# Gated cross-attention: the attention sums turned by VectorE in 32x32 blocks instead of by TensorE

## The reference

```python
Q = query @ Wq.T + bq; K = key @ Wk.T + bk; V = value @ Wv.T + bv      # 16 heads of 16
dot = einsum('bhsd,bhtd->bhst', Q, K) / sqrt(16)
out = einsum('bhst,bhtd->bhsd', softmax(dot), V)
out = out.reshape(B, T_src, D_MODEL)        # [head, token, 16] is read as [token, 256] as it lies
return out @ Wh.T + bh
x = x + tanh(g_xattn[0]) * attention(layernorm(x), ctx)
x = x + tanh(g_ffn[0]) * ffn(layernorm(x))  # w1, w3, silu, w2 plus two experts of rank 16 per token
```

## Time and profile before

| | us |
|---|---|
| median of 3 runs | 506.98 (505.81 to 508.72) |
| the profiled execution | 509.6 |
| its span in the trace | 507.7 |
| PE busy | 487.7 (96%) |
| DVE busy | 357.9 (70%) |
| ACT busy | 266.6 (53%) |
| POOL busy | 282.4 (56%) |

### The profile page before, as it was taken

One profiled execution on the slowest core, in us unless ns is written; L12 is line 12 of the kernel. 1 busy time (PEld: TensorE's weight loads), 2 busy tenths in 40 slices (PEclk: granted clock), 3 DMA queues, 4 the chain that ended last, 5 costly groups with the idle time before them and its releaser, 6 DMA issues.

```text
span 507.7 us, 11754 instructions
## 1 busy us (share of the span) xinstructions
PE 487.7 (96%) x4350; PEld 456.2 (90%) x4350; DVE 357.9 (70%) x768; ACT 266.6 (53%) x584; POOL 282.4 (56%) x339
## 2 busy tenths in 40 slices
PE   7888999999999999999899999999999999999996
PEld 6657999999999999997789999899999999999994
DVE  6866777877878877888577869856486456854444
ACT  4456766666676777667666533443335333233331
POOL 5645666666666666561676536644386444854440
PEclk9989999999999999999989999999999999999999
DMA  7793786677777777553601000010000100001001
GB/s 199 180 289 93 216 214 153 157 182 190 189 179 180 180 176 169 120 111 57 204 10 17 1 0 1 1 34 0 1 0 2 34 1 1 0 2 34 0 1 32
DMA packets 51144, 45.83 MB, mean 90 GB/s; under 512 B 33935, under 2 KB 40115, under 8 KB 51088
## 3 DMA queue, kind: packets, MB, share of 16 engines
q1 hardware_dynamic: 41310, 23.18, 19.6%
q0 software_dynamic: 7504, 18.69, 14.1%
q10 hardware_dynamic: 2274, 3.21, 2.0%
HBM read 20.59 MB, written 6.66 MB: 54 GB/s over the span
## 4 chain that ended last, share of the span: by engine, by line
PE 84%; DVE 6%; DMA 5%; issue 2%; ACT 2%; POOL 1%; ACTq 0%; DVEq 0%
PE bank L1368 14%; PE bank L1223 7%; PE bank L1246 7%; PE bank L1372 7%; PE bank L1385 6%; PE bank L1420 6%; PE bank L1205 6%; PE bank L1259 6%; PE bank L1193 5%; PE bank L1400 4%; DMA QS<-crow 3%; PE bank L1292 3%; PE bank L1403 2%; PE bank L1180 2%; PE bank L1335 2%
## 5 line engine op out<-in xcount | busy, mean ns | idle before, releaser
L970 DVE TENSOR_REDUCE nmax<-bank 100x1 f32<-100x361 f32 x256 | 130.0, 529 | 38.4 <-PE bank L1223 33.4
L419 POOL TENSOR_TENSOR awl<-hb,awh 128x400 fp32r<-128x400 f32 x63 | 70.2, 1114 | 109.4 <-ACT awh L627 109.4
L529 ACT ACTIVATE pt<-bank 120x400 f32<-120x400 f32 (+1 forms) x192 | 90.3, 503 | 25.8 <-PE bank L1246 12.2
L627 ACT ACTIVATE awh<-hb 128x400 fp32r<-128x400 f32 x64 | 34.5, 539 | 119.0 <-DVE hb L906 118.7
L1223 PE MATMUL bank<-KS,QS 96*100 96x362 f32 x256 | 86.9, 358 | 5.2 <-DVE nmax L970 4.8
L899 DVE TENSOR_TENSOR hb<-sil,bank 128x400 f32<-128x400 f32 x64 | 36.5, 570 | 73.7 <-PE bank L1385 37.9
L1246 PE MATMUL bank<-QS,KS 97*120 97x200 f32 (+1 forms) x384 | 66.4, 271 | 1.6 <-ACT pt L529 1.0
L1246 PEld LDWEIGHTS bank<-QS,KS 97*120 97x120 f32 (+1 forms) x384 | 60.2, 184 | 2.8 <-DMA QS<-crow 1.7
L328 POOL TENSOR_TENSOR cth<-craw,cth 128x724 fp32r<-128x724 f32 x16 | 27.7, 1729 | 63.0 <-ACT cth L475 54.8
L1223 PEld LDWEIGHTS bank<-KS,QS 96*100 96x100 f32 x256 | 41.6, 167 | 12.8 <-DVE nmax L970 7.3
L333 POOL DMA_DIRECT2D QS<-q_dram x90 | 46.0, 519 | 0.4 <-issue 0.3
(11 more groups left out here) (221 smaller groups left out, 1116.3 us busy)
## 6 DMA issues: line engine op xcount, KB each, us to landing
KS<-kn SPq DMA_DIRECT2D x128, 90.5 KB, 3.3
KS<-kn POOLq DMA_DIRECT2D x64, 90.5 KB, 3.4
craw<-ctxT POOLq DMA_DIRECT2D x14, 361.0 KB, 4.9
QS<-q_dram POOLq DMA_DIRECT2D x92, 50.0 KB, 3.6
q_dram<-qn ACTq DMA_DIRECT2D x4, 400.0 KB, 4.1
o_dram<-on SPq DMA_DIRECT2D x16, 100.0 KB
xr<-o_dram SPq DMA_DIRECT2D x16, 100.0 KB
y<-xs SPq DMA_DIRECT2D x8, 200.0 KB
```

The source lines that it names most:

```text
L419: nc.gpsimd.tensor_tensor(awl[:, g % 2, slot], hb[:, slot], awh[:, g % 2, slot].bitcast(F32), ALU.subtract).then_inc(m["p_awl"], 1)
L529: nc.scalar.activation(pt[0:TW[t], u, :], pT[u % 3][0:TW[t], 0:CS], ACT.Exp, scale=float(DH) ** -0.5).then_inc(m["act_e"], 1)
L970: nc.vector.tensor_reduce(nmax[:, h // 8, pos % 8:pos % 8 + 1], pS[h % 2][0:S, 0:T], AX.X, ALU.max, negate=True).then_inc(m["dve_s"], 1)
```

## The change

TensorE's four transposes and ScalarE's copy in front of them go. In their place VectorE turns the bank `pO` itself, in 13 blocks of 32 columns for each group of 32 partitions, one instruction of 128 x 416 (`blocks_turned`), and divides afterwards in the layout that this gives: partition = (group of four heads, column within the block), block, value. For this the heads are renamed: the sum of head 4g+q now stands in group g, so that the 400 columns of one group are 400 consecutive entries of the list (head, token), and 16 of them make one row of `xr`. A 13th block is only half used (columns 400 to 415 of `pO`, set to 1 once at the start). `xr` has 104 rows of which 4 mean nothing, its even and odd rows are read by two DMAs, and `turned_o` copies in two instructions that put the columns back in order. The DMA that fills `xr` from the bias in step 0 becomes eight. The core of the diff (places are named, numbers of lines left out):

```diff
@@ storage
-        o_dram = nc.dram_tensor("o_dram", [B, H * S, DH], F32, kind="Internal").ap()
+        o_dram = nc.dram_tensor("o_dram", [B, OC, 128, DH], F32, kind="Internal").ap()
...
-        osb = sba("osb", [128, NQ, S])
-        rz = sba("rz", [S, H])
-        on = sba("on", [S, H, DH])
-        xr = sba("xr", [S, D])
+        oT = sba("oT", [128, OC, 32])
+        rz = sba("rz", [128, OC])
+        on = sba("on", [128, OC, DH])
+        xr = sba("xr", [4 * RG, D])
@@ sync: body
-                    sp.dma_start(o_dram[i - 1].rearrange("(h s) d -> s h d", h=H), on[:]).then_inc(m["xo"], 16)
+                    sp.dma_start(o_dram[i - 1].rearrange("c p d -> p c d"), on[:]).then_inc(m["xo"], 16)
...
-                    sp.dma_start(xr[:], v_dram.rearrange("(r c) d -> r (c d)", c=H)).then_inc(m["xi"], 16)
+                    sp.wait_ge(m["xr_ok"], 1)
+                    src = v_dram.rearrange("(r c) d -> r (c d)", c=H)
+                    for half in range(2):
+                        for g in range(4):
+                            row = half * 4 * OC + OC * g
+                            sp.dma_start(xr[row:row + OC - half], src[25 * g + half:25 * g + 25:2]).then_inc(m["xv"], 16)
...
-                    sp.dma_start(xr[:], o_dram[i - 1].rearrange("(r c) d -> r (c d)", c=H)).then_inc(m["xi"], 16)
+                    for half in range(2):
+                        sp.dma_start(xr[half * 4 * OC:(half + 1) * 4 * OC],
+                                     o_dram[i - 1].rearrange("c (g h p) d -> h g c (p d)", g=4, h=2)[half]).then_inc(m["xi"], 16)
@@ scalar: body, last_step and after it (three places)
-                    wait(act, "pe_pv", i * UN)
-                    wait(act, "pe_oT", i - 1)
-                    nc.scalar.activation(osb[:].rearrange("p q s -> p (q s)"), pO[:, 0:CS], ACT.Copy).then_inc(m["act_o"], 1)
@@ vector: start
+            nc.vector.memset(pO[:, 0:OC * 32], 1.0).then_inc(m["pO_ok"], 1)
+            nc.vector.memset(xr[:], 0.0).then_inc(m["xr_ok"], 1)
@@ vector
+            def blocks_turned(i):
+                dve.wait_ge(m["pe_pv"], i * UN)
+                wait(dve, "dve_on", i - 1)
+                nc.vector.transpose(oT[:].rearrange("p c d -> p (c d)"), pO[:, 0:OC * 32]).then_inc(m["dve_o"], 1)
...
-                nc.vector.reciprocal(rz[:].rearrange("p (h o) -> p h o", o=1), o3[:, :, DH:VW]).then_inc(m["dve_rz"], 1)
+                dve.wait_ge(m["dve_o"], i)
+                nc.vector.reciprocal(rz[:].rearrange("p (c o) -> p c o", o=1), oT[:, :, DH:VW]).then_inc(m["dve_rz"], 1)
...
-                nc.vector.tensor_copy(ot[:].rearrange("p k s -> p (k s)"), pP[1][:, 0:KT * S]).then_inc(m["dve_ot"], 1)
+                for half in range(2):
+                    nc.vector.tensor_copy(ot[:].rearrange("p k (g s) -> p k g s", g=4)[:, :, :, half:25:2],
+                                          pP[1][:, 0:KT * 4 * RG].rearrange("p (k h g c) -> p h k g c", k=KT, h=2, g=4)[:, half, :, :, 0:OC - half]).then_inc(m["dve_ot"], 1)
@@ vector: body
+                if has_o(i):
+                    blocks_turned(i)
                 head(i + 1, 0)
@@ vector: last_step
+                blocks_turned(i)
+                shares(i)
+                quotient(i)
                 logits(0)
                 best_two(0)
-                shares(i)
-                quotient(i)
@@ vector: first block of the feed-forward part
                 gated(g, 0)
                 if g == 0:
+                    blocks_turned(B)
                     shares(B)
                     quotient(B)
@@ tensor: pv_unit, on_turn
-                    wait(pe, "act_o", b)
+                    wait(pe, "dve_o", b)
...
-                    last = mm(pO[32 * g:32 * g + VW, q * S:(q + 1) * S], va[0:TW[t], b % 3, t, 4 * q + g, :],
+                    last = mm(pO[32 * g:32 * g + VW, q * S:(q + 1) * S], va[0:TW[t], b % 3, t, 4 * g + q, :],
...
-            def o_turn(i):
...
-                for q in range(NQ):
-                    last = nc.tensor.transpose(pP[1][0:S, q * 128:(q + 1) * 128], osb[:, q, :], ident[:])
-                last.then_inc(m["pe_oT"], 1)
...
-                    last = nc.tensor.transpose(pP[1][:, j * S:(j + 1) * S],
-                                               xr[:, j * 128:(j + 1) * 128], ident[0:S, 0:S])
+                    last = nc.tensor.transpose(pP[1][:, j * 4 * RG:(j + 1) * 4 * RG],
+                                               xr[:, j * 128:(j + 1) * 128], ident[0:4 * RG, 0:4 * RG])
@@ tensor: body
                 st_unit(i, 2)
-                if has_o(i):
-                    o_turn(i)
                 st_unit(i, 3)
...
-                if has_o(i):
-                    pe.wait_ge(m["dve_on"], i)
+                if has_k(i):
+                    pe.wait_ge(m["dve_kl"], KT * b + 1)
@@ host: order of the rows of Wq, Wk
-    order = np.arange(D).reshape(4, KT, 2 * DH).transpose(1, 0, 2).reshape(-1)
+    order = np.arange(D).reshape(KT, 2, 4, DH).transpose(0, 2, 1, 3).reshape(-1)
```

More of the change, by code:

```diff
@@ L29 @@
 CS = 4 * S
+OC = 13
+RG = 2 * OC
 NC = B // 4
@@ L696, in last_step @@
                 expo(i, 0)
-                act.wait_ge(m["pe_pv"], i * UN)
-                act.wait_ge(m["pe_oT"], i - 1)
-                nc.scalar.activation(osb[:].rearrange("p q s -> p (q s)"), pO[:, 0:CS], ACT.Copy).then_inc(m["act_o"], 1)
                 expo(i, 1)
@@ L725, in _ @@
             last_step(B - 1)
-            act.wait_ge(m["pe_pv"], B * UN)
-            act.wait_ge(m["pe_oT"], B - 1)
-            nc.scalar.activation(osb[:].rearrange("p q s -> p (q s)"), pO[:, 0:CS], ACT.Copy).then_inc(m["act_o"], 1)
             for g in range(NC * FT):
@@ L1634, in _ @@
                 up(g, 1)
-                if g == 0:
-                    o_turn(B)
                 if g == 1:
```

28 lines of the change are left out of this document (10 added, 18 removed).

## The result

The changed kernel took 512.49 us (median of 4 runs, 510.55 to 514.24), the kernel before 506.55 beside it: ratio 1.009, 95% interval 1.0055 to 1.0125. The prediction was 506.8, its range ended at 511.5. In a second batch the same kernel took 513.53, ratio 1.0132 (1.0104 to 1.0159). The profiled execution was 511.39 us with a span of 509.6; it answers to the 509.6 and 507.7 of before.

A forecast was written before the change was run, and what follows sets the result against it. PE, 84% of the chain, was taken as the bound; +0.3, -1.0, +0.7, -0.1, -0.4 and +0.3 summed to -0.2 us, from the 506.98 median to 506.8. Own range 504.6 to 509.2, widened for 8 in 10 to 503.0 to 511.5.

The forecast's parts named there:

- I count all of these as nothing: Extra DMA issues and pieces delaying xr, step 0's eight DMAs, on_turn's 104 rows, turned_o, memsets and shorter quotient: priced at 0.
- The rival on the row send: Wait for the row send doesn't shrink, xr reads being two DMAs; 0.3 us longer in ten steps: 510.8 us, chance 0.12.
- Step 14, "-0.1": Step bound by VectorE and PE in turn: first head 0.20 later, PE 0.44 less, half hidden anyway: -0.1 us.
- Steps 12 and 13, +0.34 each: VectorE itself late there, so the block transpose's whole 0.51 us reach PE, less 0.17 won: +0.34 us each, +0.7.
- The plain step, +0.03: Steps 1 to 11: 0.20 us lost before s_head 2, 0.17 won from PE's transposes: +0.03 each, +0.3.
- in full: Rival: PE's four transposes count wholly, 0.44 us a step instead of 0.17: 503.0 us, chance 0.13.
- hidden: Rival: VectorE's block transpose costs nothing because head 0 has more room; 0.17 a step won: 504.0 us, chance 0.10.
- double time: Rival: VectorE's block transpose takes 1.01 us, making head 0 0.61 late: +5.8, 512.6 us, chance 0.18.
- The row send, -1.0: Wait before unit 6 in steps 1, 5 and 8: row lands 0.26 us earlier, PE arrives 0.03 later: -1.0 us.
- The last step, -0.4: VectorE's additions precede the router wait; ScalarE's expo 3 waited 0.42 us for PE, so transposes count nearly in full: -0.4.
- The first feed-forward block, +0.3: Feed-forward block 0: block transpose stands between gated and the reciprocal, so turned_o ends later and delays y_proj: +0.3 us.
- the memsets: Two at the start, 1.0 us at most, before 2.03 us of VectorE waiting for the context: counted as nothing.

The follow-up runs named there:

- experiment 1: Changed kernel with xr read back by one contiguous DMA of 104 rows instead of two scattered ones: 508.94 us, 1.0031; again 510.09, 1.0069.
- experiment 2: Kernel before with its read-back as two DMAs of 48 rows in the changed kernel's scattered pattern, last four rows left out: 509.8 us, 1.0059.
- experiment 3: Changed kernel with xr read back by two DMAs of 52 rows each, both contiguous: 509.53 us, 1.0037.
- experiment 8: One-read kernel with four identity turns (0.44 us together) added on PE behind st_unit 2, read by nothing: 512.1 us, 1.0108.
- experiment 7: One-read kernel with VectorE turning only one 32-column block of the 13: 507.37 us, 1.0008.
- one-read kernel: Changed kernel with one contiguous DMA of 104 rows for the read-back of xr, the kernel of experiment 1: 508.94 us, again 510.09.
- the spread: Kernel before with 13 small VectorE root-arithmetic instructions moved from the ends of steps 11 and 12 (0-based) to where VectorE waits for PE: 506.3 us, 0.9984.
- experiment 11: One-read kernel with six identity turns on PE early in step 14, where PE waits for VectorE: 508.71 us, 1.004; granted clocks of all runs compared.

## Why the prediction was wrong, by its own steps

- **The step that failed:** "Two more DMA issues on SP and 64 more pieces of 64 bytes on the way to `o_dram` delay `xr`, which PE reads most of a step later ... I count all of these as nothing." The cover was taken as the distance to the read, a step; but `xr` landed up to 9.1 us into the step before, and PE wants it at 9.8. With the reads scattered it lands at 11.3. Priced at 0, measured at 3.5 us (experiments 1, 2 and 3). The rival on the row send named "two DMAs now", took their number for the cause and gave 510.8 at a chance of 0.12; it is their order, and in both profiles of the changed kernel waits for `xr` make step 4 long, in the second step 5 too.
- **Step 14, "-0.1": it is +0.45 (13.54 for 13.09).** Its own terms, 0.20 later and half of 0.44 less, make -0.02, and that part held: the quotient starts as early as before. What failed is that the quotient would "become shorter by 0.05": beside GpSimd's instruction it takes 0.86 us for 0.41. The chains show where the time lies; that the move of its operand from PSUM to SBUF is the reason is argued from the 16 places, no run takes it back.
- **Steps 12 and 13, +0.34 each: right.** 14.25 and 14.02 for the forecast 14.3 and 14.1 (+0.30 and +0.30).
- **The plain step, +0.03: right** within 0.04 (13.22). The turn at 0.60 was 0.616, head 0 came 0.23 later for 0.20; PE won 0.21 where 0.17 was read from `expo` 2 and `k_low` 1. The rivals "in full" and "hidden" are out by experiments 8 and 7, "double time" by the 0.616. Of the two estimates drawn from the Trainium skill ("VectorE: DVE Perf Modes", "The three transpose paths") the one with the fixed part taken out, 0.68, came nearer than 1.01; that VectorE is the faster of the two paths is not so here: 0.616 us against 0.44 for PE's four turns.
- **The row send, -1.0: right where nothing else is late.** It is issued 0.23 us earlier in every step, and in the one-read kernel none delays PE by more than 0.1 in steps 1 to 11. Those eleven steps take 145.8 and 146.3 us there, 146.9 to 147.1 in the three profiles of the kernel before that leave the read-back alone (with the spread in one). In the changed kernel one long flight takes more than that back in the first profile, none in the second.
- **The last step, -0.4: as far as can be told, right.** Without a drop of the clock it takes 13.22, 13.28, 13.47 and 13.83 us with the block turn, 13.59, 13.71 and 14.07 without.
- **The first feed-forward block, +0.3: right in size.** From the end of the last step on, profiles take 249.4 to 250.3 us with the block turn and 249.2 to 249.6 without. `y_proj` stood 0.31 us for `ot` (two of the four profiles without the block turn show 0.23 and 0.33 there, so this wait isn't the change's alone):

```profile
271.12 1.11 PE L1293 MATMUL bank<-wh,ot 128*100 128x256 f32 x4 [0.31 <-DVE ot L961]
```

- **Also counted as nothing:** the memsets. VectorE's first statistics start 0.8 us later (5.64 for 4.84), and the first `pv_unit` of profiles with an undisturbed start stands at 53.75 to 53.98 us for 53.10 to 54.04: at most some 0.5 us. The eight DMAs of step 0 delay step 1 in some profiles (0.44 us here, by `xr<-v_dram`, in the chain above).

The sum by steps, on the one-read kernel and apart from the clock: up to +0.5 at the start, -0.6 to -1.3 in steps 1 to 11, +0.6 in steps 12 and 13, +0.45 in step 14, some -0.4 in the last step and +0.3 behind it, together between -0.4 and +0.9. The forecast of -0.2 and the 0.5 us by which runs with a like clock differ (experiment 11) both lie in it. The medians stand 1.8 and 2.6 us above the kernel before. So the forecast missed two things: 3.5 us for the order of the reads, and some 2 us that go with a lower granted clock, which none of its terms holds. Open stay: what lowers the clock more often, and what in the scattered order costs.

## What to carry to other kernels

"PE reads it a step later" is no slack: take the landing time in the profile, not the issue, and subtract it from the time at which the reader comes; here that was 0.7 us in the worst step before. When a layout is changed for a compute engine's sake, keep each DMA that someone awaits in an order that was seen to land early (here contiguous at both ends), and pay for the order in an access pattern of an engine that has room (here `turned_o`). Saving time on the busiest engine is worth only what its next producer allows, half here. When an operand moves from PSUM to SBUF, read the instruction's time in every stage, not its mean: beside a busy GpSimd it doubled here. And compare the granted clock of two kernels before their times.

## What the runs showed of the hardware

- A VectorE block transpose of 128 x 416 float32 from PSUM takes 616 ns, 128 x 32 takes 216: 1.04 ns an element, as for a plain copy from PSUM here, and 0.18 us fixed, for 0.15.
- A VectorE `tensor_tensor` of 128 x 208 with both operands in SBUF takes 0.37 us, and 0.86 and 1.04 us in the two places where a GpSimd `tensor_tensor` runs beside it; of 128 x 256 with the large operand in PSUM it takes 0.41 to 0.43, also beside the first of these.
- The trace has 14 landing entries for a contiguous read of 52 or 104 rows, 11 for the 100 rows of before and 5 for a scattered half; issue to landing is 4.1 us on average for a scattered half (8.19 at most), 2.8 for a contiguous one (4.9) and 3.2 for the single read (6.78). I take the 5 as a spread over fewer DMA engines, which no run tests.
- The row send's mean flight over steps 1 to 11 is 4.82 us before and 3.81 with 104 contiguous rows, though the bytes are 4% more.
